# Table phase of a graph kernel: one 64-row product of 50 columns for each node of a pair, in place of one 128-row product of 100 columns

## What is computed

```python
# round 3: attention over the edges; a term depends on the two nodes alone,
# so what a pair of nodes adds is its number of edges times one term
row_sum = jax.ops.segment_sum(e, src, num_segments=n)
num = jax.ops.segment_sum(e[:, None] * h[dst], src, num_segments=n)
# round 4: weighted neighbours
msg = hw[src] * sym_norm[:, None]
agg = jax.ops.segment_sum(msg, dst, num_segments=n_nodes)
out = jax.nn.relu(agg + b)
```

## Time and profile before

| what | us |
|---|---|
| median of 3 runs (lowest to highest) | 6365.92 (6350.64 to 6380.14) |
| the profiled execution, its own time | 6326.68 |
| its span in the profile | 6324.9 |
| PE, PE weight loads, DVE, ACT, POOL busy | 3936.2, 3153.8, 2950.9, 1293.0, 1487.3 |
| mean granted TensorE clock, share of full speed | 0.822 |

### The profile page before, as it was taken

The page is one execution under the profiler, slowest core; times in us unless marked ns, Lnnn a source line. Parts: engine busy times, 40 slices in busy tenths (PEclk is TensorE's granted clock), DMA queues, the critical chain, the costliest instruction groups (busy, mean ns, idle before and its releaser), DMA issues. The chain is left out here.

```text
span 6324.9 us, 58537 instructions
## 1 busy us (share of the span) xinstructions
PE 3936.2 (62%) x18711; PEld 3153.8 (50%) x18712; DVE 2950.9 (47%) x4400; ACT 1293.0 (20%) x2002; POOL 1487.3 (24%) x1200
## 2 busy tenths in 40 slices
PE   1056777343433344435997259995477549779999
PEld 1036777232322233324775147773466438667777
DVE  8637777466666666652112421114588620231111
ACT  0003444000000000002322023331476400022222
POOL 0130000788888888850000300000000000000000
PEclk9988888666767666666998569996799869879999
DMA  0022332555555555543000330001533244310000
GB/s 3 11 87 96 153 137 126 178 156 156 153 157 154 159 151 153 156 126 114 13 17 29 106 74 9 17 4 46 113 98 95 92 145 164 113 44 8 8 8 8
DMA packets 285470, 575.00 MB, mean 91 GB/s; under 512 B 75014, under 2 KB 194076, under 8 KB 275212
## 3 DMA queue, kind: packets, MB, share of 16 engines
q0 software_dynamic: 85312, 268.80, 14.8%
q1 hardware_dynamic: 185612, 222.76, 10.6%
q10 hardware_dynamic: 14400, 81.93, 3.9%
HBM read 438.66 MB, written 134.72 MB: 91 GB/s over the span
## 5 line engine op out<-in xcount | busy, mean ns | idle before, releaser
L1191 PE MATMUL gnn_p_msg<-gnn_msg,gnn_ident 128*128 128x264 f32 x1872 | 675.0, 537 | 1038.9 <-DVEq L1273 1038.9
L1123 POOL DMA_INDIRECT gnn_got<-kv,gnn_index x936 | 1204.5, 1287 | 295.5 <-issue 284.5
L1191 PEld LDWEIGHTS gnn_p_msg<-gnn_msg,gnn_ident 128*128 128x128 f32 x1872 | 503.8, 276 | 1209.9 <-DVEq L1273 1087.2
L651 DVE SCALAR_TENSOR_TENSOR ffn_acc<-ffn_pC,ffn_gates,ffn_acc 128x256 f32<-128x256 f32 x550 | 245.0, 480 | 1250.5 <-PE ffn_pC L535 1250.5
L535 PE MATMUL ffn_pC<-ffn_wc,ffn_h 128*128 128x256 f32 x3000 | 698.0, 392 | 13.0 <-DVE ffn_acc L640 13.0
L505 PE MATMUL ffn_pA<-ffn_all_xT,ffn_wa 128*128 x2400 | 669.9, 436 | 6.3 <-ACT ffn_h L455 6.3
L535 PEld LDWEIGHTS ffn_pC<-ffn_wc,ffn_h 128*128 128x128 f32 x3000 | 591.8, 198 | 105.3 <-DVE ffn_acc L640 20.6
L505 PEld LDWEIGHTS ffn_pA<-ffn_all_xT,ffn_wa 128*128 128x128 f32 x2400 | 459.6, 192 | 198.1 <-issue 10.2
L1253 DVE TENSOR_TENSOR gnn_prod<-gnn_got,gnn_q 128x2048 f32<-128x2048 f32 x117 | 268.7, 2297 | 432.0 <-DMA gnn_got<-kv,gnn_index 330.4
L455 ACT ACTIVATE ffn_h<-ffn_pA,ffn_hb 128x256 f32<-128x256 f32 (+1 forms) x560 | 294.3, 527 | 836.0 <-PE ffn_pA L505 836.0
L1813 PE MATMUL gnn_p_sum<-gnn_hs,gnn_edge 128*128 x2500 | 324.6, 285 | 157.5 <-DVE gnn_edge L1844 157.3
(11 more groups left out here) (311 smaller groups left out, 4118.8 us busy)
## 6 DMA issues: line engine op xcount, KB each, us to landing
weight_table<-tables_weight_slab SPq DMA_DIRECT2D x13, 3200.0 KB, 9.2
count_table<-tables_count_row SPq DMA_DIRECT2D x13, 3200.0 KB, 10.2
gnn_slab<-weight_table ACTq DMA_DIRECT2D x25, 1600.0 KB, 6.9
gnn_cell<-count_table ACTq DMA_DIRECT2D x50, 576.0 KB, 3.8
ffn_x<-x SPq DMA_DIRECT2D x30, 640.0 KB, 4.3
gnn_got<-kv,gnn_index POOLq DMA_INDIRECT x936, 3.7
gnn_cell<-count_table ACTq DMA_DIRECT2D x25, 448.0 KB, 3.4
kv<-qkv_og SPq DMA_DIRECT2D x5, 1280.0 KB, 5.1
```

What stands on the lines that cost most here:

```text
L1123: pool.indirect_dma_start(out=got[st][:, r, :], out_offset=None, in_=kv_dram, in_offset=rows_at(index[u][:, j * R + r:j * R + r + 1]))\
L1191: last = nc.tensor.matmul(p_msg[:, 0:MSG], ident[:], msg[v][:, r].rearrange("p h d -> p (h d)"), start=(r == 0), stop=(r == R - 1))
```

## The change

Each row now has two products, one for each node: weights are the 64 partitions of that node's slots in `hot`, 64 by 128, and the moving operand the same 64 partitions of `spread`, 50 columns (25 of count, 25 of weight). The first node's products go to the one PSUM bank of the tile `p_pair`, the second's to the other. The shift of the second node's columns (`second`) is gone, and `spread` has 50 columns for a row instead of 100. ScalarE's copies move as many elements from other places.

```diff
-    HALF = CHUNK // 2
...
-        second = s.sb("second", [P, 1])
...
-        spread = s.sb("spread", [P, P, 2 * BOTH])
+        spread = s.sb("spread", [P, P, BOTH])
...
-                dve.memset(second[0:P // 2, :], 0.0)
-                dve.memset(second[P // 2:P, :], float(TILES))
...
-                    dve.tensor_scalar(high_c[:], p_slot[:, P:2 * P], second[:, 0:1], None, ALU.add)
+                    dve.tensor_copy(high_c[:], p_slot[:, P:2 * P])
...
-                    dve.tensor_tensor(spread[:, :, 0:BOTH], across_tiles(high_c[:], P, BOTH), counting(P, BOTH),
+                    dve.tensor_tensor(spread[:, :, 0:TILES], across_tiles(high_c[:], P, TILES), counting(P, TILES),
                                       ALU.is_equal)
                     dve.drain()
-                    dve.tensor_tensor(spread[:, :, BOTH:2 * BOTH], spread[:, :, 0:BOTH], across_tiles(w_c[:], P, BOTH),
+                    dve.tensor_tensor(spread[:, :, TILES:BOTH], spread[:, :, 0:TILES], across_tiles(w_c[:], P, TILES),
                                       ALU.mult)
...
                         for r in range(CHUNK):
-                            at = p_pair[c % 2][:, r // HALF, r % HALF * 2 * BOTH:(r % HALF + 1) * 2 * BOTH]
-                            last = nc.tensor.matmul(at, hot[c % 2][:, r, :], spread[:, c * CHUNK + r, :], start=True, stop=True)
+                            for half in range(2):
+                                at = slice(half * SLOTS, (half + 1) * SLOTS)
+                                last = nc.tensor.matmul(p_pair[c % 2][:, half, r * BOTH:(r + 1) * BOTH], hot[c % 2][at, r, :],
+                                                        spread[at, c * CHUNK + r, :], start=True, stop=True)
...
-                        of = p_pair[c % 2][:, :, 0:HALF * 2 * BOTH].rearrange("p b (r n) -> p n b r", r=HALF)
-                        act.activation(count_slab[:, :, at].rearrange("p n (b r) -> p n b r", b=2), of[:, 0:BOTH], ACT.Copy)
-                        act.activation(weight_slab[v][:, :, at].rearrange("p n (b r) -> p n b r", b=2),
-                                       of[:, BOTH:2 * BOTH], ACT.Copy).then_inc(pairs_read, 1)
+                        of = p_pair[c % 2][:, :, 0:CHUNK * BOTH].rearrange("p b (r n) -> p b n r", r=CHUNK)
+                        act.activation(count_slab[:, :, at].rearrange("p (b n) r -> p b n r", b=2), of[:, :, 0:TILES], ACT.Copy)
+                        act.activation(weight_slab[v][:, :, at].rearrange("p (b n) r -> p b n r", b=2), of[:, :, TILES:BOTH],
+                                       ACT.Copy).then_inc(pairs_read, 1)
```

## The result

The changed kernel takes 6602.28 us (median of 4 runs, 6598.1 to 6608.64) against 6365.0 before: ratio 1.0372, 95% interval 1.0357 to 1.0386, slower by 237 us where 107 faster was forecast.

A forecast was written before the change was run, and what follows sets the result against it. The float32 load of 128 weight columns, 111.7 ns a step, was taken as the products' beat, alternating with VectorE. 6326.7 - 86.7 (`spread`) - 20 (clock) + 0 (products) = 6220 us profiled, 6259 on the median; range 6225 to 6650.

The forecast's parts named there:

- Products: TensorE's table products: 3328 more loads and matmuls, taken to cost 0, with bounds of 0 and 372 us.
- `spread`: Two VectorE instructions a pair fall from 6400 to 3200 elements, each to 3.49 us, saving 86.7 us in all.
- Loads of the two halves side by side: In the products, loads on partitions 0 to 63 and 64 to 127 run in parallel, so extra loads cost 0.
- The slower rival: Loads in series: both halves' weight loads queue in the products, chunks take 3.57 us, 6600 to 6655 us; chance 0.27.
- The sign of a wrong forecast: Products' pace per row over 223 ns by more than a few per cent, or a new wait before L1555 or L1507.
- The series price: Cost of 3328 extra loads in the products if they queue at 111.7 ns each: 372 us.
- Clock between the bouts: Shorter `spread` lets products start before the granted clock falls in some pairs: 20 us gained, two thirds of 31.8.
- My upper bound: The clock gain if products avoid the low clock in all of 12 pairs: 31.8 us.
- "Nor is issue": In the products, issue sets no limit: 32 steps can be issued in 1.28 us of a chunk's 1.787.
- ScalarE, the stores, the end of the phase: ScalarE's copies stay under its idle time, stores fit inside the shorter period, and the final wait is unchanged.

The follow-up runs named there:

- e8: The kernel before with filler identity products in TensorE's gaps, 31 after the last transposes: 6295.67 us, ratio 0.9956.
- e7: e5 with filler identity products in TensorE's gaps between bouts of products: 6238.28 us, ratio 0.9806.
- e1: The changed kernel with each 64-row product streaming 100 columns instead of 50, the surplus overwritten: 6262.56 us against 6328.23, ratio 0.9893.
- e3: The changed kernel with both products of a row on partitions 0 to 63, 50 columns: 7276.74 us, single run.
- e2: The kernel before with each 128-row product streaming 50 columns instead of 100: 6638.54 us, single run.
- e5: e1 with TensorE's loop over single pairs instead of two pairs written out: 6273.85 us against 6359.78, ratio 0.9861.
- e6: The changed kernel with TensorE's loop over single pairs, nothing else: 6559.20 us, ratio 1.0313.
- e9: e7 with the changed kernel's 50 moving columns in place of 100: 6489.11 us, ratio 1.026.

## Why the prediction was wrong

**The step that failed** is "Products": that "moving work is no limit", and so halving it cost nothing. It was costed at the full clock throughout. The moving columns were indeed hidden behind the loads, but they kept the clock up; with 50 in place of 100 the step went from 111.7 ns at 2.4 GHz to 213 a step at 1.2, two steps side by side. That is +289 us in the profile, where I had 0. I read the clock only where it was low and never asked what in the products kept it at 1.00, nor put it among the rivals. The phase came out 338 us over the one forecast (625.5 - 86.7 - 20 = 519): these 289, the 20 of the clock term below, and 28 of waits for issue make up all but 1. The Trainium skill, TensorE: Matmul & The Clock Gate, Why this matters for your kernels, advises to keep TensorE continuously busy to reach the full clock; I leaned on no more than that either. Here 41 of 41 us busy at 0.50 show that it isn't enough.

Point by point:

- *`spread`*: 3.49 us each as worked out from two sizes; 86.7 forecast, 88 measured between e8 and e7. Right.
- *Loads of the two halves side by side*: right. e1 has twice the loads in the same 1.79 us, e3 shows that they queue on one half. The two pages of the Trainium skill that the prediction cites for this, TensorEngine Tiling (Array Packing), Key Properties, and TensorE: Matmul & The Clock Gate, The mechanism, agree with the runs in that both overlap, in float32 too. The second page's 4 ns between starts are somewhat short: in the traces of the changed kernel and e1 the two products that overlap start mostly 6 or 7 ns apart, and 3 to 14 at the extremes. A load by its columns and not its partitions, LDWEIGHTS (loading the stationary operand) there, agrees as well: 213 ns at 1.2 GHz with 64 partitions (e3) and with 128 (e2).
- *The slower rival*: it foretold 6600 to 6655, and 6602 was measured, for another cause. Its mark, chunks 3.57 us apart, was nearly met (3.41); only the clock beside it tells them apart. That the time fell into its range is chance. The sign of a wrong forecast, a pace per row over 223 ns, showed too: 3.41 us for 8 rows are 427. The series price of 372 us belongs to loads that don't queue here.
- *Clock between the bouts*: I took 20 us of gain. In e5, where the rest is right, the clock still falls in 11 of 12 pairs, 7.3 to 8.8 us after `spread` starts, products take 28.8 to 31.9 us, and the phase is 15 over the 520 forecast. My upper bound was real only with fillers (e7: 507.4). The term was too large; with the transposes alone between the bouts the clock fell, and with fillers beside them it held.
- *"Nor is issue"*: true for the rate within a stream, wrong for the loop. I never counted the code. The doubled body is fetched again at the jump back, beside the stores: 25 us in the changed kernel (e6), 37 in e1.
- *ScalarE, the stores, the end of the phase*: unchanged, as said.

What stays open: what exactly the clock follows. The runs give its level for six combinations of rows, columns and halves, and no rule between them. Nor is it tested whether a fetch at the jump back is as long without the stores beside it.

## What to carry to other kernels

Moving columns hidden behind weight loads are not idle work: take them away and the clock can go, so for any edit that thins out a TensorE stream ask what level of clock the thinner stream will have, and test it with padding columns, which cost nothing while the loads are the beat (here, up to 100 columns). Products on separate halves of the partitions, writing to separate banks, gave twice the loads in the same time as long as the clock held. When a loop body's instructions double, look at the wait for issue at its jump back and shorten the written-out part.

## What the runs showed that I had not expected

- The granted clock falls from 1.00 to 0.50 in the midst of a stream that keeps TensorE busy without a gap (changed kernel, second pair, at 620; e9, between 580 and 582), and padding that does nothing of use takes 285 us off the phase (856.8 to 571.7).
- 12 filler products a pair, 312 matmuls of TensorE over the phase, took 27 us off (534.6 to 507.4); 1066 in e8 took 30 off the kernel before.
- In e1 five waits for issue at jumps back cost 7 us each, while DMA moved some 400 GB/s.
